# One scan for two blocks of channels, with another choice of turned tiles for ScalarE, in a two-layer Mamba stack

## The chip, the core and the metric

The kernel runs on one core of a Trainium2 chip. The metric is the device time of one execution in microseconds, from the launch to the end of the last instruction. Lower is better. All data are float32.

## The reference, cut to what matters

A sequence of 8192 tokens of 512 features goes through a layer norm, two Mamba blocks, a residual, and then a soft mixture of experts. Only the Mamba blocks are touched here. In each of the two layers, with 1024 channels and 16 states per channel:

```python
dA  = exp(einsum('bld,dn->bldn', delta, A))            # A = -exp(A_log)
dBu = einsum('bld,bln,bld->bldn', delta, Bm, u)
def step(h, inp):                                       # along the 8192 tokens
    dA_t, dBu_t, C_t = inp
    h = dA_t * h + dBu_t
    return h, einsum('bdn,bn->bd', h, C_t)
...
y = (ys + u * Dp) * silu(z)
```

## The kernel before, in words

**Chunks, groups, slots.** Each layer is cut into 16 chunks of 512 tokens (`T`), so there are 32 chunks `G`, one after the other. The channels are 8 blocks of 128 partitions, in two halves of 4 blocks (`HB`). In a chunk there are 32 groups `k`: for each half, its 16 states. A group has 4 slots, one per block, so a chunk has 128 slots `s`, and 64 pairs `p` of two slots. The state at the end of a chunk is carried to the next chunk through `h_last`.

**What one slot holds.** ScalarE makes `decay` = exp(delta * A) for one block and one state (128x512, into one of 4 banks of PSUM, `DEC_RING`). GpSimd makes `bu` = w * B for two blocks (128x1024, once per pair, a ring of 3, `BU_RING`); B's row is loaded into `b_rep`, broadcast over the partitions, once per group by the queue of SyncE. VectorE runs the recurrence over 512 tokens with one scan instruction. Its start value is a column of `h_last` (of zeros in the first chunk of a layer). `scanned` counts the finished scans. ScalarE may write a decay once the scan four slots earlier is done, and GpSimd a `bu` once both scans three pairs earlier are done.

**Turning.** When the four scans of a group are done, TensorE transposes the group into four tiles of tokens by channels, `("state", k, j)` with j from 0 to 3. Tile j of group k - 1 is turned in slot 4k + 1 + j. There are two banks for turned tiles (`TURNS`), used in turn by all tiles in program order: the 128 state tiles, 8 `skip` tiles (u * D, slots 7, 4, 5, 8 and 31, 33, 35, 38) and 8 `y` tiles (the finished sums turned back, slots 116, 118, 120, 122 and 22, 25, 27, 29). So a tile can only be turned when the tile two before it has been read. A state tile is multiplied by C (`c_now`) and added up. Either VectorE does both at once on `acc` (`add_state`, line 1182), in the slot in which the tile is turned, right after that slot's scan; or ScalarE writes the product to `prod` two slots later (`product`, line 871), and GpSimd adds these products up in pairs. `V_AT` says which tile of an even and of an odd state is ScalarE's: one tile of every four. Skip tiles are copied to `acc` by ScalarE (`copy_skip`, line 878), also two slots after their slot, and the first `add_state` on such a tile of `acc` waits for the copy. VectorE gates the y tiles (`gate_y`, line 1191).

**What lies around it.** The projections, the convolution, the gate and the softplus of this and the next chunk are spread over the slots by a timetable made before the launch (`WORK` for TensorE, `TAKE` for ScalarE's part). ScalarE's queue in slot s is: the decay, then `save_last`, then its products and skip copies (`V_TAKE`), then steps of the input's layer norm (`NORM_AT`, layer 0 alone), then the takes. Its long takes are the two `silu_u` (slots 43 and 65) and the two `silu_z` (slots 116 and 1 of the next chunk), each with a load of its function table before and behind it, the latter in `exp_tables`. `taps` are four small activations (line 738). GpSimd's queue has besides the 64 `bu` of a chunk: 14 pair sums and 2 joins (`SUM_AT`), and 4 sums and 4 products of delta (`W_AT`, by pair).

## Time and profile before

| | |
|---|---|
| time, median of 3 runs | 7764.41 us (7763.73 to 7766.31) |
| profiled execution, first to last instruction | 7761.4 us |
| between that span and the median | 3.0 us |
| share of the span: PE, VectorE, ScalarE, GpSimd | 91%, 95%, 76%, 85% |
| one chunk in mid-run | 221.8 us |
| stage behind the Mamba stack (experts) | 580 us |
| mean granted clock of TensorE | 0.98 |

The profile is one execution of the program, taken by the hardware profiler. The page first gives the busy time of each engine. The other views used are: groups of equal instructions with the mean duration of one; the waits, summed by who waited for whom; busy time in chosen stretches; and the instructions of one engine in order of time. There, an instruction's record reaches into the start of the next one, so the distance from start to start is the time that an instruction takes in a full queue, and it is shorter than its duration. L12 means line 12 of the kernel. PEld is TensorE's weight load.

### The profile page before, as it was taken

The numbers are of one execution on the slowest core, as the hardware profiler recorded it, in microseconds if no ns is written. First come the engines' busy times: TensorE is split into PE (matmuls) and PEld (weight loads), VectorE is DVE, ScalarE is ACT, GpSimd is POOL, SyncE is SP. The second block draws the span as 40 slices with busy tenths as digits, with TensorE's granted clock in tenths as the row PEclk, the third lists the DMA queues.
The fourth block names the chain that finished last, engine by engine and source line by source line (L and its number), as shares of the span: only waits on it lengthen the run. The fifth ranks groups of instructions, "written<-read, shape, count | busy, mean of one in ns | idle before, by whom it ended". The sixth has DMA issues, their size and how long they took to land. (4 is left out here: it accounts for less than half of the span.)

```text
span 7761.4 us, 100822 instructions
## 1 busy us (share of the span) xinstructions
PE 7045.9 (91%) x31116; PEld 4002.2 (52%) x31116; DVE 7373.2 (95%) x8275; ACT 5872.5 (76%) x11175; POOL 6604.5 (85%) x2871
## 2 busy tenths in 40 slices
PE   7899999999999999999999999999999999987799
PEld 3555555555555555554555555545555555554664
DVE  6999999999999999999999999999999999999655
ACT  7787788887877888777777777777777777775564
POOL 5999999999999999999999999999999999998010
PEclk9999999999999999999999999999999999998899
DMA  2221121112221211122211111111111111111665
GB/s 91 60 66 66 61 66 59 55 62 66 66 66 61 66 59 55 62 68 66 66 50 56 48 52 54 55 55 56 49 55 50 51 54 55 55 50 41 246 232 184
DMA packets 230984, 549.66 MB, mean 71 GB/s; under 512 B 27120, under 2 KB 27376, under 8 KB 210864
## 3 DMA queue, kind: packets, MB, share of 16 engines
q1 hardware_dynamic: 201776, 491.81, 19.9%
q10 hardware_dynamic: 28672, 51.39, 1.8%
q8 instruction: 252, 4.13, 0.2%
q14 instruction: 284, 2.33, 0.1%
HBM read 441.39 MB, written 101.71 MB: 70 GB/s over the span
## 5 line engine op out<-in xcount | busy, mean ns | idle before, releaser
L1082 POOL TENSOR_TENSOR bu<-w,b_rep 128x1024 f32<-128x1024 f32 x2048 | 4806.9, 2365 | 541.8 <-DVE h L1162 532.5
L1162 DVE TENSOR_TENSOR_SCAN h<-decay,h_last,bu 128x512 f32<-128x512 f32 x3840 | 4813.9, 1274 | 13.9 <-ACT decay L855 13.9
L591 PEld LDWEIGHTS turn<-ident_m,h 128*128 128x128 f32 x16384 | 1952.1, 142 | 2702.7 <-DVE acc L1182 1315.3
L855 ACT ACTIVATE decay<-delta,neg_a 128x512 f32<-128x512 f32 x4096 | 2777.4, 690 | 647.6 <-DVE h L1162 609.5
L591 PE MATMUL turn<-ident_m,h 128*128 128x128 f32 x16384 | 2558.2, 280 | 421.0 <-DVE acc L1182 348.2
L1182 DVE SCALAR_TENSOR_TENSOR acc<-turn,c_now,acc 128x512 f32<-128x512 f32 x3072 | 2243.7, 730 | 72.1 <-ACT c_now L883 43.1
L871 ACT ACTIVATE prod<-turn,c_now 128x512 f32<-128x512 f32 x1024 | 701.0, 685 | 504.2 <-PE turn L591 369.0
L1097 POOL TENSOR_TENSOR prod<-prod 128x1024 f32<-128x1024 f32 x448 | 1057.6, 2361 | 10.6 <-ACT prod L871 10.6
L513 PE MATMUL proj<-x_conv,w_in 128*128 128x512 f32 x2048 | 1046.3, 603 | 4.5 <-ACT x_conv L845 1.3
L513 PE MATMUL proj<-x_gate,w_in 128*128 128x512 f32 x2048 | 1019.8, 595 | 0.0
L513 PE MATMUL proj<-conv_in,conv_diag 128*128 128x512 f32 x1984 | 996.6, 594 | 0.0
L513 PE MATMUL proj<-zy,w_out 128*128 128x512 f32 x1024 | 505.6, 596 | 23.0 <-ACT u L756 20.5
L513 PE MATMUL proj<-w_out,zy 128*128 128x512 f32 x1024 | 504.4, 599 | 0.9 <-DVE zy L1191 0.9
L513 PEld LDWEIGHTS proj<-x_conv,w_in 128*128 128x128 f32 x2048 | 328.3, 193 | 123.5 <-issue 91.7
L513 PEld LDWEIGHTS proj<-x_gate,w_in 128*128 128x128 f32 x2048 | 324.1, 191 | 98.0 <-issue 91.8
L1162 DVE TENSOR_TENSOR_SCAN h<-decay,zeros_m,bu 128x512 f32<-128x512 f32 x256 | 320.1, 1272 | 46.7 <-POOL bu L1082 43.6
L513 PEld LDWEIGHTS proj<-conv_in,conv_diag 128*128 128x128 f32 x1984 | 313.8, 191 | 90.7 <-issue 89.1
L1064 POOL TENSOR_TENSOR delta<-delta,w 128x1024 f32<-128x1024 f32 x128 | 302.4, 2362 | 40.7 <-ACT w L789 40.7
L599 PE MATMUL turn<-d_diag,u 128*128 128x128 f32 x2048 | 288.6, 285 | 48.5 <-DVE acc L1182 44.2
L738 ACT ACTIVATE conv_diag<-ident_m,par 128x128 f32<-128x128 f32 x992 | 316.5, 394 | 0.4
L1071 POOL TENSOR_TENSOR w<-delta,u 128x1024 f32<-128x1024 f32 x128 | 302.5, 2363 | 0.3
L599 PEld LDWEIGHTS turn<-d_diag,u 128*128 128x128 f32 x2048 | 252.9, 194 | 74.3 <-DVE acc L1182 60.1
(161 smaller groups left out, 5690.6 us busy)
## 6 DMA issues: line engine op xcount, KB each, us to landing
b_rep<-b_rows SPq DMA_DIRECT2D x1024, 256.0 KB, 3.3
x_gate<-xt SPq DMA_DIRECT2D x32, 1024.0 KB, 7.0
xt<-stage ACTq DMA_DIRECT2D x128, 256.0 KB, 2.4
x_conv<-xt SPq DMA_DIRECT2D x31, 1024.0 KB, 6.9
x_gate<-in_x_dram SPq DMA_DIRECT2D x16, 1024.0 KB, 6.7
x_l<-in_x_dram SPq DMA_DIRECT2D x16, 1024.0 KB, 9.5
m_l<-xt SPq DMA_DIRECT2D x16, 1024.0 KB, 7.8
x<-x_l SPq DMA_DIRECT2D x16, 1024.0 KB, 6.3
```

The costliest lines, as they stand in the source:

```text
L513: mm = pe.matmul(out[0:lhs.shape[1], :], lhs, rhs, start=n == 0, stop=n == count - 1)
L591: mm = pe.transpose(out[:, b * P:(b + 1) * P], h[:, (G * GROUPS + k) % H_RING, b, j * P:(j + 1) * P], ident[:])
L599: mm = pe.matmul(out[:, b * P:(b + 1) * P], u[:, hf * HB + b, j * P:(j + 1) * P], d_diag[:, hf * HB + b, :], start=True, stop=True)
L738: act.activation(conv_diag[:, b % 2, k, :], ident[:], ACT.Copy, scale=par[:, STATES + k, b:b + 1])
L855: act.activation(decay[:, (G * SLOTS_BODY + s) % DEC_RING, :], delta[:, blk, :], ACT.Exp, scale=neg_a[:, n, blk:blk + 1]).then_inc(decay_s ...
L871: act.activation(prod[:, V_BUFFER[q], k % 2, :], turn[:, BANK[tile], :], ACT.Copy, scale=c_now[:, j, n:n + 1]).then_inc(v_done, 1)
L1064: pool.tensor_tensor(delta[:, lo:lo + 2, :], delta[:, lo:lo + 2, :], w[:, lo:lo + 2, :], ALU.add).then_inc(delta_set, 1)
L1071: pool.tensor_tensor(w[:, lo:lo + 2, :], delta[:, lo:lo + 2, :], u[:, lo:lo + 2, :], ALU.mult).then_inc(w_set, 2)
L1082: pool.tensor_tensor(bu[:, (G * PAIRS + s // 2) % BU_RING, :, :], w[:, blk:blk + 2, :], b_rep[:, g % B_RING, :].unsqueeze(1).to_broadcast( ...
L1097: pool.tensor_tensor(total, total, prod[:, V_BUFFER[q]], ALU.add).then_inc(vsum_set, 1)
L1162: dve.tensor_tensor_scan(h[:, (G * GROUPS + k) % H_RING, b, :], decay[:, (G * SLOTS_BODY + s) % DEC_RING, :], bu[:, (G * PAIRS + s // 2) % ...
L1182: dve.scalar_tensor_tensor(out, src, scalar, out, ALU.mult, ALU.add).then_inc(x_done, 1)
```

## The change

VectorE now runs one scan per pair of blocks, over 2 x 512 elements, instead of two scans of 512. The decay's first column is 0 in all four banks (a memset at the start), so the state falls to what column 0 of `bu` holds, and the scan's start value is the constant 0.0. Column 0 of `bu` must then be the first state of the chunk, with the carried state in it. It is prepared as follows: ScalarE's `x_proj` also stores the first column of B by a second DMA, the SyncE queue loads it to all partitions (`load_first`); GpSimd forms the exponent for all 16 states of a half (`first_exponent`, 128x64), ScalarE takes exp (`first_exp`), GpSimd computes the product with B, the product with `h_last` and their sum (`first_state`, three 128x64 operations); and ScalarE copies two columns of it into `bu` in front of each pair (`head`, 128x2, 64 in a chunk). The decays and `bu` are written from column 1 on. Both decays of a pair are now issued in the even slot, and the scan of a pair stands in the even slot in VectorE's queue, in front of the `add_state` of both its slots. `scanned` is raised by 2 per scan. ScalarE takes turned tile 0 of even and tile 2 of odd states, instead of 0 and 3. In GpSimd's queue `product_next` 0, `sum_next` 1 and `product_next` 1 move from pairs 51, 56, 63 to 50, 53, 57.

```diff
...
-W_AT = {13: ('sum', 2), 19: ('product', 2), 25: ('sum', 3), 27: ('product', 3), 47: ('sum_next', 0), 51:
-        ('product_next', 0), 56: ('sum_next', 1), 63: ('product_next', 1)}
+W_AT = {13: ('sum', 2), 19: ('product', 2), 25: ('sum', 3), 27: ('product', 3), 47: ('sum_next', 0), 50:
+        ('product_next', 0), 53: ('sum_next', 1), 57: ('product_next', 1)}
+
+HEAD_AT = {26: ('exponent', 1), 30: ('state', 1), 54: ('exponent_next', 0), 62: ('state_next', 0)}
+HEAD_EXP_AT = {57: ('exp', 1), 115: ('exp_next', 0)}
+BFIRST_AT = 24
...
-V_AT = (0, 3)
+V_AT = (0, 2)
+LAST_DVE, LAST_ACT = 3, 2
...
+    h_first = sb("h_first", [P, 2, STATES, HB])
+    a_first = sb("a_first", [P, STATES, HB])
+    b_first = sb("b_first", [P, STATES])
...
+    def heads_before(X, hf):
+
+        return 2 * (X - 1 - X // NC) + hf
...
+        def load_first(X):
+
+            sp.wait_ge(bfirst_stored, X * 16 + 16)
+            if X > 0:
+                sp.wait_ge(hfirst_set, 2 * X)
+            sp.dma_start(b_first[:], d["b_row_first"][X].partition_broadcast(P)).then_inc(bfirst_in, 16)
...
+                if k == BFIRST_AT and not kind.last:
+                    load_first(G + 1)
...
+            if X > 0:
+                act.wait_ge(bfirst_stored, X * 16)
...
+            act.dma_start(d["b_row_first"][X].rearrange("(n o) -> n o", o=1),
+                          xdbl[RANK:RANK + STATES, 0:1]).then_inc(bfirst_stored, 16)
...
-            act.activation(decay[:, (G * SLOTS_BODY + s) % DEC_RING, :], delta[:, blk, :], ACT.Exp,
+            act.activation(decay[:, (G * SLOTS_BODY + s) % DEC_RING, 1:T], delta[:, blk, 1:T], ACT.Exp,
                            scale=neg_a[:, n, blk:blk + 1]).then_inc(decay_set, 1)
+
+        def head(G, p):
+
+            k, pr = divmod(p, 2)
+            hf, n = divmod(k, STATES)
+            if p % (PAIRS // 2) == 0:
+                act.wait_ge(hfirst_set, 2 * G + hf + 1)
+            act.wait_ge(scanned, G * SLOTS_BODY + (2 * (p - BU_RING) + 2 + C_SCAN))
+            act.copy(bu[:, (G * PAIRS + p) % BU_RING, :, 0], h_first[:, hf, n, 2 * pr:2 * pr + 2]).then_inc(head_set, 1)
+
+        def first_exp(n):
+
+            act.wait_ge(exponent_set, n + 1)
+            act.activation(a_first[:], a_first[:], ACT.Exp).then_inc(afirst_set, 1)
...
-                    decay_of(G, kind, k, b)
+                    if b % 2 == 0:
+                        head(G, s // 2)
+                        decay_of(G, kind, k, b)
+                        decay_of(G, kind, k, b + 1)
+                    if s in HEAD_EXP_AT:
+                        what, hf = HEAD_EXP_AT[s]
+                        X = G + what.endswith("_next")
+                        if X < G_END and X % NC > 0:
+                            first_exp(heads_before(X, hf))
...
-            pool.tensor_tensor(bu[:, (G * PAIRS + s // 2) % BU_RING, :, :], w[:, blk:blk + 2, :],
-                               b_rep[:, g % B_RING, :].unsqueeze(1).to_broadcast([P, 2, T]), ALU.mult).then_inc(bu_set, 1)
+            pool.tensor_tensor(bu[:, (G * PAIRS + s // 2) % BU_RING, :, 1:T], w[:, blk:blk + 2, 1:T],
+                               b_rep[:, g % B_RING, 1:T].unsqueeze(1).to_broadcast([P, 2, T - 1]), ALU.mult).then_inc(bu_set, 1)
+
+        def first_exponent(X, hf):
+
+            blks = slice(hf * HB, hf * HB + HB)
+            pool.wait_ge(delta_set, X * HB + (2 * hf + 2))
+            pool.wait_ge(a_set, 2 * (X // NC) + 2)
+            pool.wait_ge(hfirst_set, 2 * X + hf)
+            pool.tensor_tensor(a_first[:], neg_a[:, :, blks], delta[:, blks, 0].unsqueeze(1).to_broadcast([P, STATES, HB]),
+                               ALU.mult).then_inc(exponent_set, 1)
+
+        def first_state(X, hf):
+
+            blks, fresh = slice(hf * HB, hf * HB + HB), X % NC == 0
+            pool.wait_ge(w_set, X * NB + (hf * HB + HB + C_W))
+            pool.wait_ge(bfirst_in, X * 16 + 16)
+            if X > 0:
+                pool.wait_ge(head_set, (X - 1) * PAIRS + (hf + 1) * (PAIRS // 2))
+            pool.tensor_tensor(h_first[:, hf], w[:, blks, 0].unsqueeze(1).to_broadcast([P, STATES, HB]),
+                               b_first[:].unsqueeze(2).to_broadcast([P, STATES, HB]), ALU.mult).then_inc(hfirst_set if fresh else first_step, 1)
+            if not fresh:
+                n = heads_before(X, hf)
+                pool.wait_ge(afirst_set, n + 1)
+                pool.wait_ge(hlast_set, (X - 1) * GROUPS + (hf + 1) * STATES + C_HS)
+                pool.tensor_tensor(a_first[:], a_first[:], h_last[:, hf * STATES * HB:(hf + 1) * STATES * HB].rearrange("p (n b) -> p n b", b=HB),
+                                   ALU.mult).then_inc(first_step, 1)
+                pool.wait_ge(first_step, 2 * n + 2)
+                pool.tensor_tensor(h_first[:, hf], h_first[:, hf], a_first[:], ALU.add).then_inc(hfirst_set, 1)
...
+        first_state(0, 0)
...
+                if p in HEAD_AT:
+                    what, hf = HEAD_AT[p]
+                    X = G + what.endswith("_next")
+                    if what.startswith("exponent") and X < G_END and X % NC > 0:
+                        first_exponent(X, hf)
+                    if what.startswith("state") and X < G_END:
+                        first_state(X, hf)
...
+        dve.memset(decay[:, :, 0:1], 0.0).then_inc(heads_zero, 1)
+
+        def scan(G, kind, p):
+            k, pr = divmod(p, 2)
+            dve.wait_ge(decay_set, G * SLOTS_BODY + (2 * p + 2))
+            dve.wait_ge(bu_set, G * PAIRS + (p + 1 + C_BU))
+            dve.wait_ge(head_set, G * PAIRS + (p + 1))
+            if pr == 0:
...
-            start = zeros[:, 0:1] if kind.first or kind.enters else h_last[:, s:s + 1]
-            dve.tensor_tensor_scan(h[:, (G * GROUPS + k) % H_RING, b, :], decay[:, (G * SLOTS_BODY + s) % DEC_RING, :], bu[:, (G * PAIRS + s // 2) % BU_RING, b % 2, :], start,
-                                   ALU.mult, ALU.add).then_inc(scanned, 1)
+            at = (G * SLOTS_BODY + 2 * p) % DEC_RING
+            dve.tensor_tensor_scan(h[:, (G * GROUPS + k) % H_RING, 2 * pr:2 * pr + 2, :].rearrange("p b t -> p (b t)"),
+                                   decay[:, at:at + 2, :].rearrange("p b t -> p (b t)"),
+                                   bu[:, (G * PAIRS + p) % BU_RING, :, :].rearrange("p b t -> p (b t)"), 0.0,
+                                   ALU.mult, ALU.add).then_inc(scanned, 2)
...
-                k, j = divmod(s, J)
-                scan(G, kind, k, j)
+                if s % 2 == 0:
+                    scan(G, kind, s // 2)
...
```

## Rows read from the trace of the kernel before

**Rows 1.** The page, busy time, share and instructions of each engine.

```profile
PE 7045.9 (91%) x31116; PEld 4002.2 (52%) x31116; DVE 7373.2 (95%) x8275; ACT 5872.5 (76%) x11175; POOL 6604.5 (85%) x2871
```

**Rows 2.** Stretches: span, busy time (instructions) by engine, clock, DMA share, GB/s.

```profile
2446.50:2668.30 221.80, 205.35 (x918) 115.75 (x917) 218.96 (x233) 178.93 (x345) 204.98 (x91) 0.99 0.20 63
```

**Rows 3.** The waits of VectorE over the whole span: total us, times, longest.

```profile
DVE acc L1182 <- ACT c_now L883: 43.1, 31, 1.4
DVE acc L1182 <- PE turn L591: 24.9, 49, 2.0
DVE h L1162 <- ACT decay L855: 17.1, 33, 1.9
```

**Rows 4.** Groups of instructions: busy us, mean ns of one | idle before.

```profile
L1162 DVE TENSOR_TENSOR_SCAN h<-decay,h_last,bu 128x512 f32<-128x512 f32 x3840 | 4813.9, 1274 | 13.9 <-ACT decay L855 13.9
...
L1182 DVE SCALAR_TENSOR_TENSOR acc<-turn,c_now,acc 128x512 f32<-128x512 f32 x3072 | 2243.7, 730 | 72.1 <-ACT c_now L883 43.1 <-PE turn L591 24.9 <-ACT acc L878 3.4
...
L1191 DVE TENSOR_TENSOR zy<-turn,zy 128x512 f32<-128x512 f32 x256 | 174.7, 682 | 8.8 <-PE turn L607 8.7
...
L1842 DVE TENSOR_TENSOR var_c<-mv_c,den_sq 128x2 f32<-128x2 f32 x32 | 5.2, 161 | 1.1
L1850 DVE SCALAR_TENSOR_TENSOR add_c<-mv_c,mul_c 128x2 f32<-128x2 f32 x32 | 5.1, 161 | 0.1
...
```

**Rows 5.** VectorE in order of time: start us, duration us, instruction.

```profile
3000.08 0.73 DVE L1182 SCALAR_TENSOR_TENSOR acc<-turn,c_now,acc 128x512 f32<-128x512 f32 x1
3000.72 1.27 DVE L1162 TENSOR_TENSOR_SCAN h<-decay,h_last,bu 128x512 f32<-128x512 f32 x1
...
3009.89 3.63 DVE L1162 TENSOR_TENSOR_SCAN h<-decay,h_last,bu 128x512 f32<-128x512 f32 x3
```

**Rows 6.** Groups of GpSimd's instructions.

```profile
L1082 POOL TENSOR_TENSOR bu<-w,b_rep 128x1024 f32<-128x1024 f32 x2048 | 4806.9, 2365 | 541.8 <-DVE h L1162 532.5 <-DMA b_rep<-b_rows 7.9
...
L1055 POOL TENSOR_TENSOR nmr_x<-neg_mean,rstd_x 128x4 f32<-128x4 f32 x16 | 3.4, 214 | 38.9 <-ACT rstd_x L830 38.9
```

**Rows 7.** ScalarE in order of time.

```profile
2999.92 0.21 ACT L888 COPY h_last<-h 128x4 f32<-128x4 f32 x1
3000.01 1.30 ACT L738 ACTIVATE conv_diag<-ident_m,par 128x128 f32<-128x128 f32 x4
3001.19 1.30 ACT L855 ACTIVATE decay<-delta,neg_a 128x512 f32<-128x512 f32 x2
```

**Rows 8.** Groups: half of a softplus on ScalarE.

```profile
L785 ACT ACTIVATE w<-w 128x1024 f32<-128x1024 f32 x128 | 135.8, 1061 | 0.0
```

**Rows 9.** VectorE in order of time, slots 7 and 8 of a chunk.

```profile
2543.54 0.73 DVE L1182 SCALAR_TENSOR_TENSOR acc<-turn,c_now,acc 128x512 f32<-128x512 f32 x1
...
2546.86 0.75 DVE L1182 SCALAR_TENSOR_TENSOR acc<-turn,c_now,acc 128x512 f32<-128x512 f32 x1 [1.40 <-ACT c_now L883]
```

**Rows 10.** TensorE in order of time, the same slots.

```profile
2541.48 1.02 PE L513 MATMUL proj<-x_conv,w_in 128*128 128x512 f32 x2
2542.34 0.60 PE L591 MATMUL turn<-ident_m,h 128*128 128x128 f32 x4
2542.78 1.06 PE L599 MATMUL turn<-d_diag,u 128*128 128x128 f32 x8
2544.32 0.65 PE L591 MATMUL turn<-ident_m,h 128*128 128x128 f32 x4 [0.49 <-DVE acc L1182]
```

**Rows 11.** ScalarE in order of time, the same slots.

```profile
2545.54 0.68 ACT L855 ACTIVATE decay<-delta,neg_a 128x512 f32<-128x512 f32 x1
2546.15 0.58 ACT L878 COPY acc<-turn 128x512 f32<-128x512 f32 x1
```

**Rows 12.** ScalarE in order of time, slot 43 (`silu_u`) and slot 44.

```profile
2602.98 1.28 ACT L760 ACT_TABLE_LOAD   x1
...
2607.50 1.28 ACT L738 ACTIVATE conv_diag<-ident_m,par 128x128 f32<-128x128 f32 x4
2608.68 0.67 ACT L855 ACTIVATE decay<-delta,neg_a 128x512 f32<-128x512 f32 x1
```

More of the change, by code:

```diff
@@ L378, in mamba_stack @@
     tap_set = sem("tap_set")
+    bfirst_stored = sem("bfirst_stored")
+    bfirst_in = sem("bfirst_in")
+    exponent_set = sem("exponent_set")
+    afirst_set = sem("afirst_set")
+    first_step = sem("first_step")
+    hfirst_set = sem("hfirst_set")
+    head_set = sem("head_set")
+    heads_zero = sem("heads_zero")
     block = ctx.enter_context(nc.Block())
     G_END = LAYERS * NC
+    def heads_before(X, hf):
+        return 2 * (X - 1 - X // NC) + hf
     PROLOGUE_NORMED = C_PROJ + KD + NB + KD
@@ L494, in _ @@
         load_out_weights(0)
+        load_first(0)
         for layer in range(LAYERS):
@@ L892, in _ @@
         clear_halo(0, C_PROJ)
+        act.wait_ge(heads_zero, 1)
         def first_tile(n):
@@ L1002, in body @@
                     if s == C_AT[1] and not kind.first:
-                        act.wait_ge(x_done, dve_base(G, kind) + (kind.turns.by_dve["state", GROUPS - 1, 2] + 1 + C_TURN))
-                        act.wait_ge(v_done, act_base(G, kind) + (kind.turns.by_act["state", GROUPS - 1, 3] + 1 + C_PROD))
+                        act.wait_ge(x_done, dve_base(G, kind) + (kind.turns.by_dve["state", GROUPS - 1, LAST_DVE] + 1 + C_TURN))
+                        act.wait_ge(v_done, act_base(G, kind) + (kind.turns.by_act["state", GROUPS - 1, LAST_ACT] + 1 + C_PROD))
                         take_c(1)
                     if s == C_AT[0] and not kind.last:
-                        last = "state", STATES + HALF_C - 1, 2
+                        last = "state", STATES + HALF_C - 1, LAST_DVE
                         act.wait_ge(x_done, dve_base(G, kind) + (kind.turns.by_dve[last] + 1 + C_TURN))
-                        act.wait_ge(v_done, act_base(G, kind) + (kind.turns.by_act["state", last[1], 3] + 1 + C_PROD))
+                        act.wait_ge(v_done, act_base(G, kind) + (kind.turns.by_act["state", last[1], LAST_ACT] + 1 + C_PROD))
                         act.wait_ge(proj_done, proj_base(G, kind) + (kind.place[ORDER.index(("turn_c", 0, 0))] + 1 + C_PROJ))
@@ L1102, in join @@
             pool.wait_ge(vsum_set, done)
-            last = "state", hf * STATES + STATES - 1, 2
+            last = "state", hf * STATES + STATES - 1, LAST_DVE
             pool.wait_ge(x_done, dve_base(G, kind) + (kind.turns.by_dve[last] + 1 + C_TURN))
@@ L1147, in _ @@
         dve.wait_ge(zeros_set, 4)
-        def scan(G, kind, k, b):
-            s = HB * k + b
-            dve.wait_ge(decay_set, G * SLOTS_BODY + (s + 1))
-            dve.wait_ge(bu_set, G * PAIRS + (s // 2 + 1 + C_BU))
-            if b == 0:
+        dve.memset(decay[:, :, 0:1], 0.0).then_inc(heads_zero, 1)
[5 more added lines that the diff above has]
+            if pr == 0:
                 dve.wait_ge(hlast_set, G * GROUPS + (k - H_RING + 1 + C_HS))
@@ L1944, in build @@
          "mu": mu, "gamma_t": gamma_t, "beta_t": beta_t, "scale": scale, "w1": w1, "b1": b1, "w2": w2, "b2": b2}
-    for name, shape in (("xt", [(LAYERS + 1) * NC, P, KD, T]), ("b_rows", [LAYERS * NC, STATES, T]),
+    for name, shape in (("xt", [(LAYERS + 1) * NC, P, KD, T]), ("b_rows", [LAYERS * NC, STATES, T]), ("b_row_first", [LAYERS * NC, STATES]),
                         ("x1", [NC, P, J, D_MODEL]), ("xh", [NC, P, J, D_MODEL])):
```

## The prediction

> **What bounds the kernel now.** The page comes first: VectorE is busy for 95% of the span, TensorE for 91%, GpSimd for 85%, ScalarE for 76% [rows 1]. These are averages over the Mamba stack and a stage of 580 us behind it, which the change doesn't touch. So I read one chunk [rows 2]: of its 221.8 us VectorE is busy for 219.0, TensorE for 205.4, GpSimd for 205.0, ScalarE for 178.9. VectorE is the bound, and two others are within 7% of it. The waits of VectorE [rows 3] say what it still loses: over 31 or 32 chunks 43 us for ScalarE's copies of skip tiles and C, 25 us for turned tiles, 17 us for decays, 2.7 us in a chunk. Then the groups give single durations [rows 4, 6, 8], and the order in time gives what an instruction takes in a full queue [rows 5, 7]: 0.64 us for an `add_state`, 1.18 for a scan ((3.63 - 1.27) / 2), 0.09 for a tiny copy of ScalarE, 0.61 for a decay, 1.18 for `taps`.
>
> **VectorE's gain.** A DVE instruction on 2 elements takes 161 ns, with or without a constant operand; `add_state` has a scalar read from memory and takes 48 ns more than `gate_y`, of the same size [rows 4]. So of the scan's 1274 ns, 161 are fixed, 48 the start value from memory, and 1065 the 512 elements. One scan over 1024 with a constant start is 161 + 2130 = 2291 ns, less the overlap of 0.09 us: 2.20 us, against 2 x 1.18 + 0.01 = 2.37. That saves 0.17 us x 64 = 10.9 us a chunk: VectorE is busy for 208.1. Bounds: 2.37 (nothing saved) and 2.12 (both fixed parts and the overlap saved besides); I take 2.20, because two kinds of row carry it.
> A page of the Trainium skill speaks for less: "VectorE: DVE Perf Modes", section "The TRN2 errata — SBUF-src ops pay a fixed extra latency per instruction", gives a fixed cost of 120 cycles for an operation that reads PSUM, an estimate of 0.125 us per instruction. By it 64 x 0.125 = 8.0 us a chunk would be saved instead of 10.9. No row of before shows a scan of another length.
>
> **What the change adds.** ScalarE: 64 `head` copies of 0.09 us [rows 7] and 2 `first_exp` of at most 0.3, 6.3 us, so 185.2 us. If a `head` costs the full duration of such a copy, 0.2 us, it is 12.8 more. GpSimd: 8 small operations; with 214 ns for 4 elements and 2.11 ns for each further one [rows 6] a 128x64 one takes 0.34 us, 2.7 in all, so 207.7 us. Neither is above VectorE's 208.1, but nothing is left to hide a bad order. TensorE's work is the same; in a full queue it is less than its busy time: 141 tiles of 0.44 us, 144 products of 0.86 and 8 skip tiles of 0.94 [rows 10] are 193.5 us. The second store in `x_proj` and the load in SyncE's queue hide: the load stands behind B's row for group 24, its data were stored in slot 76, and the row for group 25 behind it is wanted two `bu` (4.6 us) later.
> One Trainium skill rule speaks against the small operations: "GPSIMD Engine Reference", section "Performance pitfalls for Q7 kernels", puts a read with steps above 8 bytes at 2.9 instead of 1.9 cycles per element. Three of the four kinds read a column with steps of 2048 bytes. By it they take an estimated 0.05 us more each, under 0.5 us a chunk; no row shows such a read.
>
> **New waits, place by place** (a chunk, in slots). In the new order the `add_state` of slots s and s + 1 stand directly behind one another.
> (a) *Turned banks.* A tile needs the bank of the tile two before. In a slot with a skip or y tile that is the tile which VectorE has just read, and the scan that used to lie between is gone. Going through the tile order: after 0 us of other VectorE work for the tiles (1,0) in slot 9, y in 27, y in 29, (8,2) in 39; after 0.6 us in 23, 25, 119 and 121. The price: TensorE starts 0.05 us after the record of the add ends (2543.54 + 0.73, then 2544.32 [rows 9, 10]), its tile takes 0.65, 0.03 to VectorE, and the lost overlap of 0.09: 0.82. So 4 x 0.82 + 4 x 0.22 = 4.2 us. Before, at least one scan (1.19) covered each.
> (b) *Skip tiles at the chunk's start.* From the end of the add in slot 4: TensorE's start 0.15, tile 0.44, skip tile 0.94, tile 0.5, product 0.86, tile 0.65: 3.6 us until (0,2) can be added, against 2.20 + 0.64 = 2.84 of VectorE's own: 0.7 late. Skip tile 0 follows on TensorE, then ScalarE copies it, does `taps` 1.18, `head` and now *two* decays 1.3, and the copy of skip tile 3 (0.58): VectorE finds it 1.6 us late. Before, with one decay there [rows 11], this cost 1.4, and the tile 0.4. Now 2.3 together.
> (c) *ScalarE in slots 30 to 44.* The ring of decays allowed ScalarE 3 slots ahead; now it may start pair p when scan p - 2 is done. From the end of scan 15 to the start of scan 18, VectorE has 2 adds, scan, 2 adds, scan, 1 add: 7.6 us. ScalarE: 0.64 and 0.15 until the skip tile starts, 1.1 for it, copy 0.48, exp 0.95 (1.06 less overlap [rows 8]), `head` and decays 1.3, ln 0.94, copy 0.48, `taps` 1.18, `head` and decays 1.3, 0.1: 8.6. Wait 1.0, and 0.3 for the next pair (product, copy, conversion 0.75 and decays, 3.1 against 2.84). Then `silu_u`: from the end of scan 19 to the start of scan 22 VectorE has 8.4 us with (a)'s wait; ScalarE gets the last `conv` tile 2.3 us in, takes it (0.6), 4.52 for `silu_u` with its table loads, `taps` 1.18 [rows 12], `head` and decays 1.3 + 0.1: 10.0. Wait 1.6. Sum 2.9; before, the decays cost 0.5. `silu_z` in slot 116 fits but for 0.2.
> (d) *GpSimd, pairs 23 to 57.* 35 `bu`, 9 sums and 6 of delta's operations, 50 x 2.325 (205.0 / 88 [rows 2]) and 1.8 of small ones are 118.1 us. They may take the time from the end of scan 20 to the start of scan 57: 36 scans, 56 adds, 115.0 us, and 1.6 of (c)'s wait. 1.5 us are missing. Before, with the longer scans, these pairs fitted. Moving delta's last three operations forward makes this stretch fuller; it makes room for `first_state` in pair 62.
> The new choice of tiles itself takes no time off any engine: VectorE keeps 3 of 4. It spreads its adds 1, 2, 2, 1 over the pairs instead of 0, 2, 2, 2, which gives GpSimd and ScalarE a steadier pace.
>
> **The sum.** 208.1 + 4.2 + 2.3 + 2.9 + 0.2 + 1.5 = 219.2 us a chunk, 2.6 less than now. 32 chunks: -83 us; about +3 at the start (`first_state(0, 0)`, one more load before it). The profiled execution has 7761.4 us, 3.0 under the median, and becomes 7681; on the median's scale **7685 us**. It is a small difference of two large terms: 32 x 10.9 = 349 us of scans saved, about 270 us of new waits (11.1 less the 2.7 of now, 32 times).
>
> **Rivals.**
> *The waits are covered.* For it: the waits of (b), (c) and (d) lie near one another, and one delay gives the others room. Against it: (a) is a bare loop of two engines. If only (a) and half of the rest come, the chunk is 215.7: 7570 us. If nearly none come, GpSimd's 207.7 and VectorE's 208.1 hold the chunk at about 212: 7455.
> *Slower: ScalarE's ring is too short.* The place is every pair in which ScalarE has more than 3.2 us of work, 20 or so of 64 by the takes. `head` then costs its full 0.2 us, since it and the decay behind it wait for semaphores first, and ScalarE (198 us with that) is late again and again. It decides the sign from 13.7 us of waits in a chunk, 2.6 more than forecast; at 0.3 us more in 20 pairs the chunk is 225: 7870 us. For it: 7.6 against 8.6 in (c). Against it: ScalarE still idles for 10 to 16% of the chunk.
> *The scan saves less.* If the constant start is as slow as one from memory, 3.1 us of the 10.9 are gone; (d)'s wait goes with it, and the chunk is 220.6: 7730. This is also where the page's 120 cycles end. If the long scan saves nothing at all (two banks of PSUM in one read), the chunk is 219.0 + 8: 7930.
>
> **How the numbers follow.** A run of this kernel can tell 0.2% (16 us) from no change. My forecast, 7640 to 7730: 0.40. Waits covered, below 7640: 0.16. Scan saves less, 7700 to 7780: 0.14. Ring too short, 7780 to 7900: 0.25. Nothing saved: 0.05. The range 7590 to 7850 leaves out half of the second and the far ends of the last two, 0.2. Faster by over 0.2% (below 7749): 0.40 + 0.16 and a part of the third, 0.60. Same 0.10. Slower 0.30.
>
> **What would show it.** The scans: 2048 of 128x1024, mean 2.29 us; 2.34 says that the start's 48 ns stay, over 2.5 that the gain is none. VectorE busy 208 us in a mid chunk, and the chunk 219 us long. VectorE's waits on turned tiles: over 4 us a chunk, in records of 0.7 us. Waits of the scan on decays: 3 us a chunk, at pairs 18 and 22. On `bu`: 1 to 2 us, around pair 57. ScalarE's `head`: 0.2 us long, 0.09 from start to start. The prediction is wrong if VectorE's idle time in a chunk is under 8 or over 14 us, or if `bu`, now from an odd offset, takes other than 2.36 us.

## The result: 2.2% slower

The changed kernel takes **7934.06 us** (median of 4 runs, 7933.9 to 7936.41) against 7764.11 of the kernel before on the same chip: ratio 1.0219, 95% interval 1.0204 to 1.0233. Forecast were 7685 us and a range of 7590 to 7850.

The page of the changed kernel, its engines' busy time (answers to [rows 1]):

```profile
span 7932.1 us, 101470 instructions
PE 7027.1 (89%) x31116; PEld 4057.0 (51%) x31116; DVE 7094.6 (89%) x6228; ACT 6049.7 (76%) x13283; POOL 6677.6 (84%) x3115
```

VectorE's busy time fell by 279 us, as planned, and the span grew by 171. So VectorE idles 450 us more. One chunk of layer 0, and one of layer 1, each cut at its length (columns as in [rows 2]):

```profile
2400.00:2628.70 228.70, 206.85 (x916) 118.32 (x916) 209.77 (x168) 183.47 (x407) 206.08 (x98) 0.98 0.19 61
5000.00:5225.10 225.10, 201.87 (x900) 114.48 (x900) 209.97 (x169) 174.54 (x384) 207.04 (x97) 0.99 0.16 52
```

No engine is busy for more than 94% of a chunk any more: none sets the pace by its work alone. The groups (answers to [rows 4] and [rows 6]; below them ScalarE's decays, products and heads, and TensorE's turned tiles):

```profile
L1139 POOL TENSOR_TENSOR bu<-w,b_rep 128x1022 f32<-128x1022 f32 x2048 | 4815.1, 2365 | 632.4 <-DVE h L1256 624.3
L1256 DVE TENSOR_TENSOR_SCAN h<-decay,bu 128x1024 f32<-128x1024 f32 x2048 | 4667.7, 2279 | 231.3 <-ACT decay L889 169.6
...
L621 PE MATMUL turn<-ident_m,h 128*128 128x128 f32 x16384 | 2549.2, 280 | 493.2 <-DVE acc L1278 460.8
L889 ACT ACTIVATE decay<-delta,neg_a 128x511 f32<-128x511 f32 x4096 | 2667.7, 686 | 278.5 <-DVE h L1256 276.4
L1278 DVE SCALAR_TENSOR_TENSOR acc<-turn,c_now,acc 128x512 f32<-128x512 f32 x3072 | 2198.5, 732 | 267.6 <-PE turn L621 215.0
L919 ACT ACTIVATE prod<-turn,c_now 128x512 f32<-128x512 f32 x1024 | 702.0, 686 | 943.7 <-PE turn L621 739.9
...
L899 ACT COPY bu<-h_first 128x2 f32<-128x2 f32 x2048 | 387.0, 189 | 18.0 <-ACT conv_in L879 12.2
```

VectorE's waits (answers to [rows 3]; total us, times, longest), and of ScalarE's the first three:

```profile
DVE acc L1278 <- PE turn L621: 215.0, 434, 2.0
DVE h L1256 <- ACT decay L889: 169.6, 139, 2.5
DVE zy L1287 <- PE turn L637: 87.6, 98, 5.5
...
DVE acc L1278 <- ACT c_now L931: 49.8, 31, 1.6
DVE h L1256 <- POOL bu L1139: 45.8, 2, 44.5
```

```profile
ACT prod L919 <- PE turn L621: 739.9, 499, 4.8
ACT decay L889 <- DVE h L1256: 276.4, 222, 2.9
```

The wait on `bu` is one of 44.5 us at the start. Turned tiles and decays are what VectorE waits for: before, 25 and 17 us [rows 3]. The largest wait is one off VectorE: ScalarE's products wait 740 us for their turned tile. In the kernel before this was:

```profile
ACT prod L871 <- PE turn L591: 369.0, 376, 3.5
```

**Where in the chunk.** I gave every instruction of VectorE its slot by program order and added up the idle time in front of it, as a mean over chunks 8 to 13 (layer 0) and 20 to 27 (layer 1). The forecast is beside it, without the lost overlap that its prices in (a) contain:

| idle us of VectorE in slots | 0-19 | 20-49 | 50-95 | 96-127 | sum |
|---|---|---|---|---|---|
| before, layer 0 | 1.8 | 0.5 | 0.5 | 0.0 | 2.8 |
| forecast | 3.0 | 5.3 | 0 | 2.0 | 10.3 |
| after, layer 0 | 4.2 | 5.6 | 5.4 | 3.4 | 18.6 |
| after, layer 1 | 4.6 | 5.6 | 2.7 | 2.5 | 15.3 |

The places that were forecast in slots 0 to 49 show as forecast, within 0.4 us each. VectorE in order of time, slots 8 and 9, then two `y` tiles of slots 27 and 29:

```profile
2629.35 0.75 DVE L1278 SCALAR_TENSOR_TENSOR acc<-turn,c_now,acc 128x512 f32<-128x512 f32 x1 [1.63 <-ACT c_now L931]
2630.86 0.75 DVE L1278 SCALAR_TENSOR_TENSOR acc<-turn,c_now,acc 128x512 f32<-128x512 f32 x1 [0.75 <-PE turn L621]
...
2662.21 0.69 DVE L1287 TENSOR_TENSOR zy<-turn,zy 128x512 f32<-128x512 f32 x1 [0.75 <-PE turn L637]
...
2666.48 0.69 DVE L1287 TENSOR_TENSOR zy<-turn,zy 128x512 f32<-128x512 f32 x1 [0.75 <-PE turn L637]
```

Forecast were 1.6 for the skip tile and 0.82 for each bank (0.75 of idle time and the overlap of some 0.08). What the forecast did not have lies in three places. The first is slot 2, behind the `silu_z` of slot 1; here is VectorE's scan:

```profile
2615.52 2.29 DVE L1256 TENSOR_TENSOR_SCAN h<-decay,bu 128x1024 f32<-128x1024 f32 x1 [0.75 <-ACT decay L889]
```

The second is slots 96 to 127. The forecast's 2.0 there were 1.5 for a wait on `bu`, which never came, and 0.5 for the rest; in layer 0 VectorE waits 3.4 us there, all of it for turned tiles (mainly slots 111, 116 and 118). The third and largest is slots 50 to 95. In layer 0 the scans of slots 66 and 78 wait 1.3 and 2.0 us for decays, and turned tiles cost 2.1; in layer 1 these are 1.6, 0 and 1.2. ScalarE around the second `silu_u`, and the scan of slot 66 behind it:

```profile
2495.52 1.30 ACT L889 ACTIVATE decay<-delta,neg_a 128x511 f32<-128x511 f32 x2
2496.75 0.18 ACT L936 COPY h_last<-h 128x4 f32<-128x4 f32 x1
2496.95 1.28 ACT L790 ACT_TABLE_LOAD   x1
2498.25 1.91 ACT L790 ACTIVATE u<-u 128x2048 f32<-128x2048 f32 x1
2500.18 1.28 ACT L733 ACT_TABLE_LOAD   x1
2501.47 0.19 ACT L899 COPY bu<-h_first 128x2 f32<-128x2 f32 x1
2501.57 1.29 ACT L889 ACTIVATE decay<-delta,neg_a 128x511 f32<-128x511 f32 x2
```

```profile
2502.95 2.29 DVE L1256 TENSOR_TENSOR_SCAN h<-decay,bu 128x1024 f32<-128x1024 f32 x1 [1.26 <-ACT decay L889]
...
2524.20 2.29 DVE L1256 TENSOR_TENSOR_SCAN h<-decay,bu 128x1024 f32<-128x1024 f32 x1 [2.02 <-ACT decay L889]
```

Both decays of the pair stand behind the long take, and the scan needs both: it starts when the second is done. The second scan of these rows, in slot 78, is 2.02 us late through a row of small waits that ScalarE has in its queue, none of which looks like a cause alone:

```profile
2517.29 0.58 ACT L798 COPY xdbl<-proj 64x512 f32<-64x512 f32 x1 [0.63 <-PE proj L543]
2517.90 0.32 ACTq L800 DMA_DIRECT2D b_rows<-xdbl  x1
2518.26 0.44 ACTq L802 DMA_DIRECT2D b_row_first<-xdbl  x1
2518.74 0.16 ACT L804 COPY spare_m<-proj 128x1 f32<-128x1 f32 x1 [0.87 <-ACT xdbl L798]
2520.08 0.69 ACT L919 ACTIVATE prod<-turn,c_now 128x512 f32<-128x512 f32 x1 [1.18 <-PE turn L621]
2520.67 0.58 ACT L879 COPY conv_in<-proj 128x512 f32<-128x512 f32 x1
...
2522.72 0.19 ACT L899 COPY bu<-h_first 128x2 f32<-128x2 f32 x1 [0.41 <-ACT conv_in L879]
2522.82 1.29 ACT L889 ACTIVATE decay<-delta,neg_a 128x511 f32<-128x511 f32 x2
```

### The profile page after: what moved, and what is told of

The parts are those of the page before. It is cut to its first block and busy times, and to the rows that moved or that the text cites. A ratio compares the mean times of both kernels' runs of the same rounds, so it can differ in the third digit from the quotient of the medians.

```text
span 7932.1 us, 101470 instructions
## 1 busy us (share of the span) xinstructions
PE 7027.1 (89%) x31116; PEld 4057.0 (51%) x31116; DVE 7094.6 (89%) x6228; ACT 6049.7 (76%) x13283; POOL 6677.6 (84%) x3115
## 3 DMA queue, kind: packets, MB, share of 16 engines
q14 instruction: 289, 2.37, 0.1%
## 5 line engine op out<-in xcount | busy, mean ns | idle before, releaser
L1139 POOL TENSOR_TENSOR bu<-w,b_rep 128x1022 f32<-128x1022 f32 x2048 | 4815.1, 2365 | 632.4 <-DVE h L1256 624.3
L1256 DVE TENSOR_TENSOR_SCAN h<-decay,bu 128x1024 f32<-128x1024 f32 x2048 | 4667.7, 2279 | 231.3 <-ACT decay L889 169.6
L621 PEld LDWEIGHTS turn<-ident_m,h 128*128 128x128 f32 x16384 | 1993.2, 143 | 2702.9 <-issue 1454.0
L889 ACT ACTIVATE decay<-delta,neg_a 128x511 f32<-128x511 f32 x4096 | 2667.7, 686 | 278.5 <-DVE h L1256 276.4
L1278 DVE SCALAR_TENSOR_TENSOR acc<-turn,c_now,acc 128x512 f32<-128x512 f32 x3072 | 2198.5, 732 | 267.6 <-PE turn L621 215.0
L543 PE MATMUL proj<-conv_in,conv_diag 128*128 128x512 f32 x1984 | 1021.3, 607 | 0.9 <-ACT halo L778 0.9
L899 ACT COPY bu<-h_first 128x2 f32<-128x2 f32 x2048 | 387.0, 189 | 18.0 <-ACT conv_in L879 12.2
L637 PE MATMUL turn<-ident_m,acc 128*128 128x128 f32 x1024 | 166.9, 287 | 181.4 <-DVE acc L1278 98.8
```

The lines of the kernel that those rows point to most:

```text
L543: mm = pe.matmul(out[0:lhs.shape[1], :], lhs, rhs, start=n == 0, stop=n == count - 1)
L621: mm = pe.transpose(out[:, b * P:(b + 1) * P], h[:, (G * GROUPS + k) % H_RING, b, j * P:(j + 1) * P], ident[:])
L889: act.activation(decay[:, (G * SLOTS_BODY + s) % DEC_RING, 1:T], delta[:, blk, 1:T], ACT.Exp, scale=neg_a[:, n, blk:blk + 1]).then_inc(dec ...
L899: act.copy(bu[:, (G * PAIRS + p) % BU_RING, :, 0], h_first[:, hf, n, 2 * pr:2 * pr + 2]).then_inc(head_set, 1)
L1139: pool.tensor_tensor(bu[:, (G * PAIRS + s // 2) % BU_RING, :, 1:T], w[:, blk:blk + 2, 1:T], b_rep[:, g % B_RING, 1:T].unsqueeze(1).to_broa ...
L1256: dve.tensor_tensor_scan(h[:, (G * GROUPS + k) % H_RING, 2 * pr:2 * pr + 2, :].rearrange("p b t -> p (b t)"), decay[:, at:at + 2, :].rearr ...
```

## Experiments

All times are one run beside the kernel before (7763 to 7766 us in each set). The first question was which part of the change costs.

**Order or load.** The kernel before with the new choice of tiles and the new order (both decays in the even slot, both scans in front of the adds of two slots), but two scans of 512 and no heads:

```diff
-                    decay_of(G, kind, k, b)
+                    if b % 2 == 0:
+                        decay_of(G, kind, k, b)
+                        decay_of(G, kind, k, b + 1)
...
-                scan(G, kind, k, j)
+                if s % 2 == 0:
+                    scan(G, kind, k, j)
+                    scan(G, kind, k, j + 1)
```

> The kernel before with the new choice of tiles and the new order of the queues, but with two scans of 512 elements and no preparation of first states: both decays in the even slot, both scans in front of both adds. Theory 'order' (the new waits come from the order alone): VectorE waits at the same places as after the change, about 15 us more in a chunk than before, less some 3 us that the longer scans cover: 8150 us. Theory 'load' (the waits come from the 64 copies, the two exponentials and the second store on ScalarE): under 3 us more in a chunk, at most 7860 us.

8016.22 us, between the two forecasts and nearer to 'order'. The order (with the choice of tiles) is the cost; the long scan with its heads takes 82 us off it again. That is little: the long scans take 10.6 us a chunk off VectorE's own work (the chunk's length less idle time and lost overlaps), 340 us in all. VectorE idles 9.7 us a chunk here (8.2 in layer 1) and 18.6 (15.3) in the changed kernel, so three quarters of the gain turn into waits. This is the run's list of ScalarE's first waits: 929 us for turned tiles, against 369 in the kernel before. VectorE's scans nevertheless wait only 27 us for decays in this run.

```profile
ACT prod L871 <- PE turn L591: 929.0, 623, 4.8
ACT decay L855 <- DVE h L1164: 461.4, 375, 4.8
```

**64 small copies more on ScalarE**, in the kernel before, where `head` stands (into a buffer that nothing reads):

```diff
                     if b % 2 == 0:
+                        act.copy(heads_out[:, n % 8, :], heads_in[:]).then_inc(heads_done, 1)
```

> The kernel before with 64 copies of 128x2 in a chunk on ScalarE, one in front of each even slot's decay, into a buffer that nobody reads; everything else as before. Theory 'order': ScalarE has 43 us of idle time in a chunk and its ring of decays is four slots deep, so the time stays within 0.3% of 7764 us. Theory 'load': each copy costs its 0.19 us and delays the takes, 7764 + 32 x 5 = 7920 us.

7774.82 us, 11 more than before. In the old order ScalarE's load is not it. These copies wait for no scan as `head` does, and what the load costs in the new order no run shows.

**The choice of tiles, from both sides.** In the changed kernel back to the old choice, and in the kernel before alone:

```diff
-V_AT = (0, 2)
-LAST_DVE, LAST_ACT = 3, 2
+V_AT = (0, 3)
+LAST_DVE, LAST_ACT = 2, 3
```

> The changed kernel with the old choice of turned tiles (0 and 3). Theory 'tiles' (the new choice makes the waits on turned tiles): faster than 7934 us by 50 us or more. Theory 'order': the four places where a tile follows directly on the tile two before move, and two pairs of eight hold no add for a pair, so ScalarE and GpSimd get less time there: 7934 to 8030 us.

> The kernel before with ScalarE's tiles 0 and 2 instead of 0 and 3, nothing else. In the old slot order a scan lies between any two adds, so theory 'order' expects under 0.2% either way, 7750 to 7780 us. Theory 'tiles' (tile 2 is a worse choice in itself, since its product holds a bank that an add used to free): 30 us or more slower, as the 38 us between the changed kernel and the one with the old tiles.

7895.54 us (38.5 less than the changed kernel; neither forecast) and 7798.52 (35.5 more than the kernel before; as 'tiles' had it). In both orders the choice costs 36 to 38 us. The places don't agree: in the old order a chunk gets 1.8 us longer in layer 0 and 0.8 in layer 1, in the new one 3.7 and nothing, so the likeness of the two totals is chance. With the kernel before and only this choice at 7798.5, the new order is worth 8016.2 - 7798.5 = +218 us, and long scans with heads -82: +35.5 + 218 - 82 = 171. This is the whole difference by construction, each term being the step from one kernel to the next.

**ScalarE's part of the order**, in the kernel before: both decays in the even slot, scans and tiles as they were (the first edit above alone).

> The kernel before with one thing alone: ScalarE makes both decays of a pair of slots at the even slot. Scans stay single and in their slots, tiles 0 and 3. The whole order (scans and decays) cost 218 us over the kernel with the new tiles. If ScalarE's part of it is what costs (the second decay waits for a scan one slot sooner, and holds up products and takes behind it): 7870 to 7980 us. If VectorE's part is (two scans, then the adds of two slots behind one another): 7764 to 7800 us, and the waits of VectorE on turned tiles stay near the 25 us of before.

7817.5 us, +55: neither of the two forecasts, a quarter of the order's cost. Some 160 us are left for VectorE's part, the adds of two slots behind one another, and what the two do to each other.

**The second decay back in its odd slot**, in the changed kernel:

```diff
-                        decay_of(G, kind, k, b)
-                        decay_of(G, kind, k, b + 1)
+                    decay_of(G, kind, k, b)
```

> The changed kernel with the second decay of a pair back in the odd slot of ScalarE's queue, behind the even slot's takes. If the takes suffer because two decays and a head stand in front of them, they come 0.6 us earlier, TensorE gets its banks back sooner, and the waits on turned tiles shrink by 1 to 3 us a chunk; but the scan of the pair then waits for the odd slot's decay behind the even slot's takes, which costs up to the length of these takes where ScalarE is late. Theory 'order' with the takes as the main victim: 7870 us. With the decays as the main victim: 8000 us or more. Theory 'load': no change.

8011.58 us, +77, the forecast for decays as the main victim. The scan needs both, so the second decay sets its start; behind the takes of the even slot it is later still. Pairing the decays costs 55 us in the kernel before, and here it is needed.

**Extra tiles moved**, so that none of VectorE's operations on a turned tile follows directly on its read of the tile two before:

```diff
-Y_AT = ((116, 118, 120, 122), (22, 25, 27, 29))
-SKIP_AT = ((7, 4, 5, 8), (31, 33, 35, 38))
+Y_AT = ((116, 118, 120, 122), (22, 24, 26, 28))
+SKIP_AT = ((5, 2, 3, 4), (31, 33, 35, 37))
```

> The changed kernel with skip tiles in slots 5, 2, 3, 4 and 31, 33, 35, 37 and the y tiles of the second half in 22, 24, 26, 28, so that no add or y follows directly on the read of the tile two before. If the waits at slots 7, 8, 9, 27, 29 and 39 (5.2 us a chunk in the profile after) come from this adjacency and from the late skip copies, they vanish and nothing takes their place: 7934 - 32 x 4.5 = 7790 us. If TensorE and ScalarE are late anyway (rival 'everything is one ring'), the waits move to the next scans and the time is above 7880 us.

7832.93 us, -101, between the two forecasts. That is the largest gain of any order tried, and still 70 us behind the kernel before. The same edit with the old choice of tiles:

> The changed kernel with both things that helped it by themselves: ScalarE takes tiles 0 and 3 again (-38.5 us alone) and the extra turned tiles stand in the slots of the run that moved them (-101 us alone). If the two act at different places they add up: 7795 us, within 15. If they take away the same waits (both are about what stands beside the adds of the later slot), the second is worth little: 7825 us or more. Only below 7760 would one scan for two blocks pay.

7892.14 us: 3.4 less than with the old choice alone, which is no difference. The two edits don't add, as one forecast had it; with these slots the *new* choice is the better one, by 59 us. Which tile ScalarE takes has no price of its own, only one with a given list of slots.

**The second store** issued by SyncE's queue instead of ScalarE's:

> The changed kernel with the second store of x_proj issued from the SyncE queue (at group 22, the load at 24 as before) instead of ScalarE's. If ScalarE's queue around slot 76 is what makes the scan of slot 78 wait (2.0 us in layer 0), 0.5 us less there: 15 to 30 us less in all, 7910 us. If the store is hidden, 7934 us; if the SyncE queue now holds back a row of B, slower.

7937.82 us: no change. The scan of slot 78 waits 1.5 us instead of 2.0 in layer 0, but other waits take its place, and the chunk stays as long. The store hides, as forecast.

**Products one slot later, and one slot sooner** (`PROD_LAG` 3 in the changed kernel; 1 in the one with moved tiles and the old choice):

> The changed kernel with ScalarE's products and skip copies three slots behind their tile instead of two. In the profile after, ScalarE idles 740 us before products until TensorE has turned the tile, with the next decays behind it. If these idle times are what makes decays and takes late, one slot more removes most of them: 7850 us. If the banks are the narrower place, the later product keeps a bank longer and TensorE waits more: 7980 us or more.

> The same as the run before it in this set, with ScalarE's products one slot behind the turn instead of two. Theory 'the two turned banks are the narrow place': a bank comes free some 1.7 us sooner, as it came free later by as much in the run with three slots (+111 us): 40 to 100 us faster than its neighbour. Rival 'ScalarE is the narrow place': the product now stands at the head of ScalarE's line before its tile is turned, ScalarE waits there, and the decays behind it come later: slower than its neighbour by 30 us or more.

8045.54 us (+111) and 8121.24 (+229 against its neighbour, 7892.14). Late products hold the bank (TensorE's waits for ScalarE's products grow from 93 to 384 us); soon ones hold up ScalarE (1128 us in front of its tiles instead of 398), whose decays VectorE then awaits for 487 us instead of 152. Neither side of 2 is better.

**Rings made larger.** All of this moved work within rings. To widen one, banks of PSUM had to be freed: the kernel's eight are 4 of decays, 2 of turned tiles and 2 of projections. In the first set the decays went to SBUF. Room for them came from leaving out the gate's own weights: the gate multiplies by the output weights instead, with the same instructions and shapes. With four projection banks a tile's bank also follows the running count of tiles. So these kernels, and those of the second set, compute something else and are good for their times alone. The edit for four of both:

```diff
-    decay = ps("decay", [P, DEC_RING, T])
+    decay = sb("decay", [P, DEC_RING, T])
...
-TURNS = 2
+TURNS = 4
...
-RING = 2
+RING = 4
```

> Control for the three runs behind it. The changed kernel with the four decay buffers in SBUF instead of PSUM; room for them comes from gate weights of their own being left out (the gate tiles multiply by the output weights, which are loaded once for both layers; same instructions and shapes). Unused PSUM stays unused. If a scan takes 2.28 us from there as well: 7934 within 20. If VectorE and GpSimd hinder each other in SBUF, the scan or the product of GpSimd gets longer: each 0.1 us of a scan is 205 us of time at most.

> The control with four banks for turned tiles instead of two; nothing is moved. Theory 'banks': TensorE turns the tiles of both slots ahead, VectorE's 215 us of waits of its adds on turned tiles and 88 of its gatings fall under 80 in all, ScalarE's 740 us of waits of its products fall too, and the decays come sooner: 150 to 350 us faster than the control. Rival 'ScalarE's line' (four decay buffers, both decays at the even slot): the banks only shift the wait to the decays: under 60 us faster.

> The control with four banks for projections instead of two, two turned banks as they were. If the waits that the forecast missed come from TensorE standing in front of a projection bank that ScalarE has not emptied (slots 62 to 79 and 103 to 118, some 9 us a chunk, 290 us in all): 150 to 290 us faster than the control. If they come from the turned banks: under 50 us.

> The control with four banks of each. 'Banks': nearly all of the waits that the change brought go, a chunk comes down to VectorE's busy 208 to 211 us and 3 to 5 us of waits as before: 7934 - 32 x 12 = 7550 us, within 60 of it. 'ScalarE's line': over 7850, with decays in VectorE's list of waits at 170 us or more.

11333.33, 11332.87, 11332.02 and 11332.31 us (two banks of each, four turned, four projection, four of both): four times the same, and no answer on the rings. The control's groups show what holds it:

```profile
L1246 DVE TENSOR_TENSOR_SCAN h<-decay,bu 128x1024 f32<-128x1024 f32 x2048 | 7442.2, 3634 | 891.4 <-POOL bu L1129 374.5
L1129 POOL TENSOR_TENSOR bu<-w,b_rep 128x1022 f32<-128x1022 f32 x2048 | 7591.7, 3729 | 45.0 <-DVE h L1246 45.0
```

Scans of 3.63 instead of 2.28 us beside products of 3.73 instead of 2.37: the two engines stop each other. In order of time they take turns: two scans start 4.30 us apart (at 3009.85 and 3014.15 us), and the GpSimd operations beside them 4.31 us (3010.74 and 3015.05). A scan alone takes 2.20 from start to start and a product 2.33, 4.5 together.

In the second set ScalarE still writes its decays to SBUF, with all their waits, but nothing reads them, and the scan reads a fixed factor (0.5) from PSUM:

```diff
+    factors = ps("factors", [P, 2, T])
...
-                                   decay[:, at:at + 2, :].rearrange("p b t -> p (b t)"),
+                                   factors[:].rearrange("p b t -> p (b t)"),
```

> Control for the two runs behind it. The changed kernel; ScalarE writes its decays to SBUF with the same semaphores as before, and the scans multiply by a fixed 0.5 from two PSUM banks instead (gate weights of their own are left out for the room, as in the set before). Every instruction, shape and wait stands. One operand of the scan is in PSUM again, so it should take 2.28 us and GpSimd's product 2.36: 7934 within 25 us. If the decays' writes to SBUF alone were what slowed GpSimd and VectorE, over 9000.

> The control with four turned banks instead of two. Theory 'the turned banks are the narrow place': waits of VectorE on turned tiles (303 us with the gatings) fall under 80, and the whole is 150 to 350 us faster than the control. Rival 'ScalarE's line': the waits go over to the decays, under 60 us faster.

> The control with four projection banks instead of two. Theory 'TensorE stands in front of a projection bank that ScalarE empties late, and the turned tiles behind it come late' (the 9 us a chunk that the forecast missed): 150 to 290 us faster than the control. Rival 'the turned banks alone': under 50.

| | us | idle of VectorE, layer 0, slots 0-19 | 20-49 | 50-95 | 96-127 |
|---|---|---|---|---|---|
| control | 7939.35 | 4.7 | 5.7 | 5.4 | 2.4 |
| four turned banks | **7624.08** | 1.5 | 1.5 | 6.0 | 2.3 |
| four projection banks | 7912.73 | 4.5 | 5.7 | 5.6 | 1.7 |

The control is the changed kernel again, within 6 us. Four turned banks take 315 us off, and this run alone is under the kernel before. The time is as forecast by 'the turned banks are the narrow place'. Nearly all of the gain lies in slots 0 to 49, in layer 1 too: there the four columns go from 4.7, 5.6, 2.5, 2.5 to 0.9, 1.5, 1.8, 2.6. Its waits of VectorE, ScalarE and TensorE:

```profile
DVE acc L1270 <- PE turn L612: 101.6, 109, 2.5
DVE h L1248 <- ACT decay L880: 66.2, 52, 2.3
...
DVE h L1248 <- ACT h_last L927: 48.3, 33, 1.6
...
DVE h L1248 <- ACT bu L890: 30.6, 18, 1.8
...
DVE zy L1279 <- PE turn L628: 6.8, 4, 5.2
```

```profile
ACT decay L880 <- DVE h L1248: 554.0, 484, 2.5
...
ACT prod L910 <- PE turn L612: 218.2, 261, 2.3
```

```profile
PE turn L612 <- DVE acc L1270: 188.2, 216, 3.0
```

TensorE's wait for the bank that VectorE's add empties fell from 449 us in the control to 188, ScalarE's for its tile from 740 to 218. ScalarE now runs ahead of VectorE and waits for the ring of decays (277 to 554 us), where its time costs nothing.

Of VectorE's own waits, those directly for a turned tile fell from 294 us in the control to 108 (`acc` and `zy` lines; forecast was under 80). Those of its scans for ScalarE, which the profile puts down to decays, state copies or heads, fell from 175 to 145 only. So ScalarE's 522 us less in front of its tiles reached VectorE for the smaller part, if at all.

Is it more than the loss? No run gave the kernel before four turned banks. Its VectorE was busy for 219.0 of 221.8 us a chunk [rows 2], so at most 2.8 us a chunk, 90 in all, could go there. At least 225 of the 315 us, still more than the 170 lost, are thus waits that the kernel before does not have.

Four projection banks are worth 27 us: my reading of the trace, that TensorE in front of a full projection bank delays the tiles behind it, is wrong but for that.

## Why the prediction was wrong

**Right:** the scan. 2279 ns were measured, 2291 forecast. In order of time, an add and two scans from start to start:

```profile
3000.22 2.27 DVE L1256 TENSOR_TENSOR_SCAN h<-decay,bu 128x1024 f32<-128x1024 f32 x1
3002.42 0.72 DVE L1278 SCALAR_TENSOR_TENSOR acc<-turn,c_now,acc 128x512 f32<-128x512 f32 x1
3003.07 2.28 DVE L1256 TENSOR_TENSOR_SCAN h<-decay,bu 128x1024 f32<-128x1024 f32 x1
```

The scan takes 2.20 us, as forecast, so 0.17 are saved in a pair. The rival "the scan saves less" is out. VectorE's own work in a chunk is 228.7 less 18.6 idle, 210.1, and 26 interrupted queues cost some 0.08 of overlap each: 208.0 (forecast 208.1). The Trainium skill's fixed cost of 120 cycles per instruction ("VectorE: DVE Perf Modes", section "The TRN2 errata — SBUF-src ops pay a fixed extra latency per instruction") would have made it 8.0 saved instead of 10.9, an estimate; the rows say 10.9. It has the fixed part alone. By the rows, an estimate too, the 0.17 us are 0.10 for two start values from memory (48 ns each) and 0.07 for one fixed part of 161 ns less the overlap of 0.09.

**Right:** (a) and (b) in place and price, (c)'s three scans (slot 36: 0.6, 38: 0.4, 44: 1.65 us; forecast 1.0, 0.3, 1.6), the second store, `bu` at 2365 ns. `head`: 189 ns long, forecast 0.2. GpSimd's small operations:

```profile
L1158 POOL TENSOR_TENSOR h_first<-w,b_first 128x64 f32<-128x64 f32 x64 | 22.1, 346 | 0.1
L1148 POOL TENSOR_TENSOR a_first<-neg_a,delta 128x64 f32<-128x64 f32 x60 | 22.0, 367 | 0.0
L1164 POOL TENSOR_TENSOR a_first<-a_first,h_last 128x64 f32<-128x64 f32 x60 | 20.1, 336 | 0.0
L1167 POOL TENSOR_TENSOR h_first<-h_first,a_first 128x64 f32<-128x64 f32 x60 | 19.3, 322 | 4.7
```

Forecast were 340 ns. Two kinds read a column with long steps, not three as the prediction says (`a_first` and `h_last` lie in one piece). They take 0.01 to 0.045 us more than the others; the Trainium skill's rate for such reads ("GPSIMD Engine Reference", section "Performance pitfalls for Q7 kernels"), an estimated 0.05, is an upper end here.

**Wrong, and enough for the sign:** the list of new waits. The sum had 11.1 us; the step that failed is (c), "ScalarE in slots 30 to 44", taken as the only stretch in which ScalarE falls behind. Slots 50 to 95 had no term and cost 5.4 us in layer 0 and 2.7 in layer 1: 130 us over the 32 chunks, where the forecast had a gain of 79. The second `silu_u` is as long as the first, for which the same text works out 1.6 us, and it was simply not gone through (1.3 and 1.6 us in slot 66); nor was the `silu_z` of slot 1 (0.8 in slot 2), nor `x_proj` with its chain of small waits (2.0 in slot 78, layer 0). Slots 96 to 127 had 0.5 us without the wait on `bu` and cost 3.4 and 2.5. In layer 0: 219.2 + 5.4 + 1.2 in slots 0 to 19 + 0.3 in 20 to 49 + 2.9 less the 1.5 of (d) in 96 to 127 + 18 more lost overlaps at 0.08 = 228.9; measured 228.7. For layer 1 it is 219.2 + 1.6 + 0.3 + 2.7 + 0.5 + 1.2 = 225.5; measured 225.1. What makes these waits is shown in part. The kernel with the new order and short scans has 3.5 of the 8.8 us of slots 50 to 127 in layer 0, and 1.8 of the 5.2 in layer 1; the rest comes with the shorter scans and the heads, and no run parts these two.

**Wrong:** "The new choice of tiles itself takes no time off any engine". True of busy time; yet it costs 36 to 38 us in waits with these slots. The sum had nothing for it.

**Wrong:** (d). GpSimd was to be 1.5 us short in pairs 23 to 57; no wait on `bu` appears in a chunk. VectorE's other waits give GpSimd time; that is argued, not tested.

**Small slips in the prediction:** 64 heads at 0.2 us instead of 0.09 add 7.0 us, not 12.8, so ScalarE would have 192 us with them, not 198. And 3.1 less 1.5 is 1.6: the third rival's chunk is 220.8, not 220.6. Neither moves the forecast.

**The rival had the right number, partly by luck.** "ScalarE's ring is too short" had the side, the threshold (13.7 us) and nearly the time (7870), by the decays' ring. Of VectorE's 18.6 us of idle time in layer 0, 6.8 are waits of its scans, nearly all for decays, and 10.0 are for turned tiles (5.1 and 8.5 of 15.3 in layer 1), so its mechanism is the smaller part. With four turned banks, ScalarE's ring as it was, 315 us go. But they go in slots 0 to 49, from 10.4 to 3.1 us a chunk in layer 0 and from 10.3 to 2.5 in layer 1. The forecast had 8.3 us there, by (a) to (c). What it did not have, nearly all of the 8 us of slots 50 to 127 in layer 0 and of the 5 in layer 1, stays. So the turned banks are where most of the change's cost can be got back; they don't explain what the forecast missed. The waits of (c) in slots 36 and 38 vanish with four banks too, and that of 44 (after `silu_u`) stays at 1.5: so the first two, put down to ScalarE's work, hang on the turned banks as well.

**Open:** slots 50 to 127 keep their 8 us (layer 0) with either ring widened. The rows show ScalarE's queue there, long takes in one piece and the decays in pairs; no run took these apart, and none widened the ring of decays.

## What to carry to other kernels

Merging two instructions also takes away the place between them. Before counting its saving, list for each two-buffer ring what the work between the halves covered. Follow every engine that reads the ring, too. One off the bound can pass its wait on through what stands behind it in its queue: with products one slot sooner, VectorE's waits for decays rose from 152 to 487 us. But its idle time is no price in itself: with short scans ScalarE stood 929 us in front of its tiles, and VectorE waited 27 us for decays. When one long take has been priced, go through all takes of that length, up to the last slot. And when order after order changes the sign of a few tens of us, widen the ring, if only in a kernel that gives up part of the work, and look in which slots the time goes: the ring that gives most back need not be the one that the forecast missed.

## What the hardware showed besides

- A scan with both operands in SBUF and GpSimd's products nearly exclude one another. The page "SBUF — State Buffer" of the Trainium skill, section "SBUF: two separate sides", says that a VectorE operation with two SBUF inputs and a GpSimd operation take turns. The runs agree nearly: 88 operations of GpSimd of 2.37 us and 64 scans of 2.20 are 349 us a chunk one after the other; (11331.5 - 580) / 32 = 336 were measured, so some 13 us of it overlap. With one operand in PSUM the same scan takes 2279 ns, whether ScalarE writes its decays to PSUM or to SBUF.
- ScalarE's decay takes 717 ns when it writes SBUF, and 686 when it writes PSUM (control of the second set, and the changed kernel).
- One read across two PSUM banks costs a scan nothing that shows: 2279 ns are 161 + 2 x 1059, and the short scan's part per 512 elements was 1065.
- The issue of the second, tiny DMA takes 0.44 us of ScalarE's queue, the first 0.32 (32 issues of each).
